# Issuing an fp32 score product as narrow column tiles of TensorE

## What is computed

```python
q, k, v = (x @ W.T + b).reshape(n, 8, 32)            # one each, 256 features
e = (edge_attr @ We.T).reshape(-1, 8, 32)            # 64 attributes per edge
alpha = sum(q[dst] * (k[src] + e), -1) / sqrt(32)    # one score per edge and head
alpha = exp(alpha - max over the edges of dst)       # a softmax per target node
out = segment_sum((v[src] + e) * alpha, dst) / segment_sum(alpha, dst)
h = beta * x_r + (1 - beta) * out                    # then layer norm, feed-forward
# network, layer norm, and a shared network with four gated experts
```

## Time and profile before

| what | value |
|---|---|
| median of 2 runs | 5584.19 us |
| lowest, highest | 5583.86, 5584.52 us |
| span of the profiled execution | 5584.0 us |
| mean granted clock of TensorE | 0.907 |
| PE busy | 5115.2 us, 92% |

### The profile page before, as it was taken

The page is one execution under the profiler, slowest core; times in us unless marked ns, Lnnn a source line. Parts: engine busy times, 40 slices in busy tenths (PEclk is TensorE's granted clock), DMA queues, the critical chain, the costliest instruction groups (busy, mean ns, idle before and its releaser), DMA issues. The chain is left out here.

```text
span 5584.0 us, 76757 instructions
## 1 busy us (share of the span) xinstructions
PE 5115.2 (92%) x22479; PEld 3611.0 (65%) x22479; DVE 1934.3 (35%) x4447; ACT 2257.3 (40%) x4140; POOL 1895.7 (34%) x2013
## 2 busy tenths in 40 slices
PE   4899999999999999999999999999999677877778
PEld 2577777777777777777777677777776454544545
DVE  3233233233333333333333332322333445445454
ACT  2344444444444444444444444444444323233233
POOL 1444444444444444444444444444443000000000
PEclk9899999999999999999999999999999877788778
DMA  2333333333333333333333433433433100000000
GB/s 102 94 103 96 96 100 98 97 98 94 102 96 96 103 95 95 102 92 95 103 95 95 105 94 92 104 93 96 103 94 86 61 13 20 13 13 20 13 13 7
DMA packets 486457, 445.39 MB, mean 80 GB/s; under 512 B 359613, under 2 KB 389310, under 8 KB 486408
## 3 DMA queue, kind: packets, MB, share of 16 engines
q0 software_dynamic: 96384, 265.00, 17.4%
q1 hardware_dynamic: 390024, 179.92, 12.8%
HBM read 431.89 MB, written 12.82 MB: 80 GB/s over the span
## 5 line engine op out<-in xcount | busy, mean ns | idle before, releaser
L494 POOL DMA_INDIRECT F<-xn_rows,srci x1970 | 1865.8, 947 | 2283.6 <-PE pZ L763 1799.4
L622 ACT ACTIVATE FT<-ring 128x256 f32<-128x256 f32 x1970 | 1196.9, 653 | 2328.9 <-PE ring L691 2327.2
L763 PE MATMUL pZ<-F,PT 128*128 128x321 f32 x3920 | 1380.7, 434 | 0.0
L699 PE MATMUL pS<-FT,G 128*128 128x320 f32 x3144 | 1096.0, 474 | 78.0 <-ACT FT L622 77.6
L699 PEld LDWEIGHTS pS<-FT,G 128*128 128x128 f32 x3144 | 613.0, 205 | 371.4 <-issue 202.2
L546 DVE COPY PT<-pPT 128x384 f32<-128x384 f32 (+1 forms) x786 | 348.8, 485 | 1327.8 <-PE pPT L706 1327.8
L691 PEld LDWEIGHTS ring<-ident,F 128*128 128x128 f32 x3940 | 481.5, 141 | 493.8 <-ACT FT L622 221.9
L691 PE MATMUL ring<-ident,F 128*128 128x128 f32 x3940 | 775.7, 282 | 7.4 <-DMA F<-xn_rows,srci 6.3
L763 PEld LDWEIGHTS pZ<-F,PT 128*128 128x128 f32 x3920 | 668.5, 191 | 105.0 <-issue 1.6
L539 DVE TENSOR_REDUCE nmx<-pS 128x1 f32<-128x640 f32 x393 | 324.0, 824 | 940.0 <-PE pS L699 935.3
L699 PE MATMUL pS<-F,G 81*128 81x320 f32 x1572 | 585.0, 454 | 0.0
(11 more groups left out here) (180 smaller groups left out, 3975.2 us busy)
## 6 DMA issues: line engine op xcount, KB each, us to landing
F<-in_edge_attrT SPq DMA_DIRECT2D x394, 160.0 KB
F<-in_edge_attr SPq DMA_DIRECT2D x394, 160.0 KB, 3.8
F<-xn_rows,srci POOLq DMA_INDIRECT x1970, 2.8
F<-in_dst SPq DMA_DIRECT2D x394, 42.5 KB
srci<-in_src SPq DMA_DIRECT2D x395, 2.5 KB, 3.3
x_all<-in_x SPq DMA_DIRECT2D x1, 6272.0 KB, 22.1
xn_rows<-xs SPq DMA_DIRECT2D x7, 896.0 KB, 3.9
xnb<-xn_rows SPq DMA_DIRECT2D x7, 896.0 KB, 4.8
```

The costliest lines, as they stand in the source:

```text
L494: pool.indirect_dma_start(out=F[s][:, t, 0:D], out_offset=None, in_=xn_d, in_offset=bass.IndirectOffsetOnAxis(ap=srci[j % GB][:, t:t + 1], ...
L622: act.activation(dst, src, ACT.Copy).then_inc(ring_emptied, 1)
L699: m = pe.matmul(pS[:, q, 0:SH], G[0:(P if k < KD else K3), k, j, :], f, start=(k == 0), stop=(k == 2))
L763: z = pe.matmul(pZ[:, 0:ZW], PT[:, t, :], F[s][:, t, 0:ZW], start=(t == 0), stop=(t == T - 1))
```

## The change

The score product is cut along its 128 output columns (heads and nodes). For the feature chunks (k = 0 and 1) each matmul becomes four of C = 32 columns, for the third chunk two of 64. Each writes the PSUM partitions that belong to its columns, so a piece at partition 32 uses the columns from 32 on of the array. The moving operand, 320 edges, is the same for all pieces of a chunk.

```diff
                                     f = FT[j % 2][:, k, q * SH:(q + 1) * SH] if k < KD else F3[s][0:K3, q * SH:(q + 1) * SH]
-                                    m = pe.matmul(pS[:, q, 0:SH], G[0:(P if k < KD else K3), k, j, :], f,
-                                                  start=(k == 0), stop=(k == 2))
+                                    wc = C if k < KD else 2 * C
+                                    for c in range(0, P, wc):
+                                        m = pe.matmul(pS[c:c + wc, q, 0:SH], G[0:(P if k < KD else K3), k, j, c:c + wc], f,
+                                                      start=(k == 0), stop=(k == 2))
                             m.then_inc(s_done, 1)
```

## The result

The changed kernel takes 5765.75 us (two runs, 5765.35 and 5766.14) against 5584.19: ratio 1.0326, 95% interval 1.0296 to 1.0356. The direction was right. The size was not: 7350 had been forecast, and the range began at 6850. The case that came true is "side by side", to which the prediction gave 0.13 and 5879 us; that price too was 113 us above the measured time. All ratios here compare fast executions; one of the ten of e9 was in a slower state (6072.25 us at a clock of 0.802).

What follows compares the result with a forecast made beforehand. TensorE (PE) was taken to bound the attention loop. Slots 5.90 + closing slots 1.08 + switches 0.75 = 7.73 us, less 3.24, gives 4.49 per pass; times 393 is 1765, so 5584 + 1765 = 7349, about 7350 us; range 6850 to 9640.

Steps and rivals of the forecast that it cites:

- side by side: Rival for narrow tiles in a scores pass: a chunk's four tiles share one's time; 5879 us, chance 0.13.
- PE is the bound, added time goes one for one to the end: Attention loop: PE has no slack, busy 4018.5 of 4100 us, so time added there lengthens the whole run equally.
- A narrow half streams as long as a full one, 0.27 us, with its load covered: Scores pass: each narrow half streams the same 320 columns, 0.27 us with its load covered, 0.32 without.
- The staircase: 24 slots: Scores pass: next tile's first half starts with this tile's second; 20 + 4 = 24 slots for 12; 7350 us, chance 0.55.
- Bare loads in the slots: Scores pass: 20 slots priced at 0.295 us, the middle of 0.27 (load covered) and 0.32 (bare), together 5.90 us.
- The change of width, 0.15 us each, five per pass: Scores pass: five switches of tile width, each costing drain plus bare load, 0.15 us, together 0.75 us.
- The clock: Attention loop: today's half-clock stretches cost the same after the change; a rival had it falling further, 10390 us, chance 0.04.
- Not slower: Rival for the scores pass: tiles run side by side and width switches cost nothing; 5584 us, chance 0.03.

Runs made afterwards that it cites:

- e9: The changed kernel with all three chunks in 32-column tiles, the program of e2 run again on another chip: 5588.50 us, 1.0012 times the kernel before.
- e10: The changed kernel with feature pieces ordered by tiles instead of by chunks, the program of e3 run again: 5763.26 us, 1.0331 times the kernel before.
- e11: The changed kernel with all four pieces of each feature chunk writing the first 32 partitions, thus on the same columns: 8260.79 us, 1.4800 times the kernel before.
- e12: The changed kernel with the second half's chunks ordered third, first, second, so four changes of width instead of five: 5732.22 us, 1.0266 times the kernel before.
- e6: The changed kernel with all three chunks in 64-column tiles, the program of e1 run again on another chip: 5587.56 us, 1.0002 times the kernel before.
- e1: The changed kernel with all three chunks in two tiles of 64 columns, first job: 6418.88 us, 1.1456 times the kernel before.
- e2: The changed kernel with all three chunks in four tiles of 32 columns, first job: 6556.05 us.
- e3: The changed kernel with each half's feature pieces ordered by tiles instead of by chunks, third chunk last, first job: 6584.49 us.

## Why the prediction was wrong, step by step

- **PE is the bound, added time goes one for one to the end.** Right, once the clock is counted. In the table the sum is within 13 us of the span wherever the signals came on time, 19 for the kernel with 2676 us more. DVE, ACT and POOL only waited longer.
- **A narrow half streams as long as a full one, 0.27 us, with its load covered.** Right: 16 halves of 320 columns on the same columns take 4.40 us. The Trainium skill (TensorE: Matmul & The Clock Gate, Part 3) lets a load overlap running matmuls only where the row group differs, which would bare each of the loads. As the load in the earlier trace rows did, the eight loads in 0.26 us disagree.
- **The staircase: 24 slots.** Wrong, and this is the step that failed: the forecast has 12 slots too many, 12 x 0.27 = 3.24 us per pass, x 393 = 1273 of the 1585 us by which it missed. The prediction said that the next tile's first half can start only with the second half of the tile ahead. I had taken from rows in which all matmuls use the same columns that halves start only in the order of issue. Those rows can't show otherwise: on the same columns order and necessity are one. In the changed kernel the four tiles of a chunk take the slots of one: four first halves start within 0.05 us of each other, ahead of the first tile's second half, although that one was issued before three of them. e10 shows that even three waiting halves are passed over, and e11 that it is the columns that hold a piece back. The Trainium skill (TensorE: Matmul & The Clock Gate, Part 3) has both the gain of packed column tiles, with which this trace agrees (12576 narrow records in 1092.1 us, 3144 full ones in 1096.0), and matmuls that start in program order. With the latter the trace of e10 doesn't agree; I took it as the stronger.
- **Bare loads in the slots** (0.295 for 0.27): the same step; there is one bare load per change of width, not per tile. 20 x 0.025 = 0.5 us per pass, 197 us, on top.
- **The change of width, 0.15 us each, five per pass.** The size was right: 0.15 for the one that e12 takes out. But the one into the pass is all but hidden. PE waits 0.2 us for ACT there anyway, and the first narrow load is shorter than the full one that stood bare at this place, so the pass starts faster (in the earlier trace rows the first four records take 1.16 us, not 4 x 0.27 = 1.08; so a pass before was 3.31 us, and not the 3.24 of the prediction). The one out of the pass is dearer, 0.10 of drain and 0.10 of bare load, as the load is of 128 columns. Together 0.60 for 0.75: 59 us too much.
- **The clock.** That the added time leaves the half-clock stretches as they are was wrong by 58 us, and no case of the prediction had time given back. With 0.60 for 0.75 and 58 us back, the 5879 of the side-by-side case becomes 5762. The four wrong terms, 1273 + 197 + 59 + 58 = 1587 us, account for the 1585 us of the miss.
- **Chances.** The side-by-side rival was priced well and weighed badly. Four cases rested on one unknown, and for its most likely value I had an inference, while a measured gain that the prediction itself quotes stood against it. With side by side taken in, the range would have begun at 5879, and even then the measured 5765.75 would have been below it, by the two terms just named.
- **Not slower** needed switches under 0.057 us. They cost 0.12 on average here. With two of them instead of five the kernel is within 0.2% of before, with the help of the clock.

## What to carry to other kernels

In this kernel, cutting a matmul that already fills the columns into narrow tiles gained nothing, and pieces on different columns cost nothing that could be seen. What costs is each change of tile width, so do all pieces of a stretch at one width (e6 against the changed kernel: 0.42 us per turn, 165 us at full clock, for three switches; 186 us between the two medians of that job). An order seen among instructions that compete for one resource says nothing about instructions that don't: before a forecast rests on it, ask whether any row could have shown the opposite. And where the granted clock dips at a fixed place of a loop, a longer turn can get back part of its cost (58 of 236 us in the changed kernel, 26 of 177 in e12, all of it in e6), so hold the mean clock of two traces side by side before a difference is explained.

## What the runs showed of the hardware

- Column tiles run at one time in fp32, four of 32 or two of 64: 16 halves of 320 columns take 1.22 us with the drain (changed kernel), 8 halves of 64-wide tiles 1.10 (e6), and 16 on shared columns 4.40 (e11). Tiles issued behind three waiting matmuls and their loads start ahead of them (e10: 16 halves in 1.24 us).
- A change of width costs about 0.10 us behind the end of the stream and then a bare load, about 0.03, 0.05 and 0.10 us for 32, 64 and 128 columns. From the rows of the changed kernel: the second stretch of 64 takes 0.69 us (2070.18 to 2070.87), which is 2 x 0.27 + 0.05 + 0.10, and the first pair of `pZ` behind it covers 0.81 instead of 0.70.
- On one of the chips the signals of PE's matmuls came late in kernels with narrow tiles: e1 took 6418.88 us there and 5587.56 on another, e2 6556.05 and 5588.50, e3 6584.49 and 5763.26, with passes that agree to 0.01 us. The starts of PE's next records did not wait; the signals did, by 1.5 us in the middle turns of e1, 2.5 of e3, 3.1 of e2, in 342 of 393 passes of each. They came in time in the pass behind each node block, most of which runs at half clock. In these three the clock also fell more often in the loop: 80 times in e1, 70 in e2, 105 in e3, and 49 in the kernel before. The kernel before lost little there (5606.86 against 5583.32 and 5582.94 in the other jobs). The cause stays open, and so does whether it is the chip or the moment.
